# Decoder layer, tree attention: where the softmax sum is divided out, and which engine moves weights and attention row

## What is computed

```python
self_logits = jnp.einsum('bhnd,bhnd->bhn', Q, K) * scale
nbr_logits = jnp.einsum('bhld,bhlnd->bhln', Q, nk) * scale
nbr_logits = jnp.where(causal_mask[None, None], -jnp.inf, nbr_logits)
all_logits = jnp.concatenate([self_logits[..., None], nbr_logits], axis=-1)
w = jax.nn.softmax(all_logits, axis=-1)
all_v = jnp.concatenate([V[:, :, :, None, :], nv], axis=3)
out = jnp.einsum('bhln,bhlnd->bhld', w, all_v)
...
return out @ Wo.T + bo
```

## Time and profile before

| what | value |
| --- | --- |
| median of 3 runs | 2362.91 us (2362.0 to 2380.96) |
| the profiled execution | 2362.72 us, span 2360.7 us |
| busy, of the span | TensorE 2049.5 us, VectorE 1616.1, ScalarE 1072.2, GpSimd 1036.9 |
| VectorE's waits for gathered rows, 1220 to 2300 us | 128.6 us in 92 waits |

### The profile page before, as it was taken

One profiled execution on the slowest core, in us unless ns is written; L12 is line 12 of the kernel. 1 busy time (PEld: TensorE's weight loads), 2 busy tenths in 40 slices (PEclk: granted clock), 3 DMA queues, 4 the chain that ended last, 5 costly groups with the idle time before them and its releaser, 6 DMA issues.

```text
span 2360.7 us, 33037 instructions
## 1 busy us (share of the span) xinstructions
PE 2049.5 (87%) x11360; PEld 1023.6 (43%) x11360; DVE 1616.1 (68%) x2129; ACT 1072.2 (45%) x1854; POOL 1036.9 (44%) x1084
## 2 busy tenths in 40 slices
PE   4899999999999999996147888998989999988997
PEld 2333333333333333331014555555555555555555
DVE  8564647566564647552568888888888888888850
ACT  3354545455555545464013444444444444444444
POOL 3232534244352535233444464465555555455420
PEclk9999999999999999998568999999999999999999
DMA  5442434434342434331875675665665675675520
GB/s 193 146 126 73 144 97 131 145 108 152 121 149 79 142 96 130 117 108 63 311 268 186 220 235 188 220 231 199 221 236 195 215 255 195 206 249 195 199 85 18
DMA packets 188800, 392.40 MB, mean 166 GB/s; under 512 B 20692, under 2 KB 82260, under 8 KB 188632
## 3 DMA queue, kind: packets, MB, share of 16 engines
q1 hardware_dynamic: 133336, 188.91, 25.1%
q0 software_dynamic: 55296, 201.35, 24.6%
HBM read 312.33 MB, written 77.59 MB: 165 GB/s over the span
## 4 chain that ended last, share of the span: by engine, by line
DVE 28%; DMA 11%; POOL 5%; issue 4%; PE 3%; ACT 0%; DVEq 0%; SPq 0%; ACTq 0%; POOLq 0%
DMA nb<-kv_flat,idx_rows 10%; DVE bank L1497 10%; DVE logits L1444 5%; POOL nb L1568 5%; DVE nb L1493 5%; DVE nb L1435 4%; PE bank L1172 1%; PE bank L1148 1%; DMA own<-kv_flat 1%; DVE bank L1503 1%; DVE logits L1448 1%; DVE own L1439 1%; DVE total L1474 1%; DVE top L1466 1%; DVE weights L1481 0%
## 5 line engine op out<-in xcount | busy, mean ns | idle before, releaser
L712 DVE TENSOR_REDUCE neg_max<-rows_ps 128x2 f32<-128x1024 f32 x256 | 312.4, 1220 | 298.3 <-PE rows_ps L499 298.2
L1568 POOL DMA_INDIRECT nb<-kv_flat,idx_rows x384 | 366.6, 955 | 138.0 <-issue 86.2
L1435 DVE TENSOR_TENSOR nb<-nb,bank 128x1024 f32<-128x1024 f32 x192 | 231.7, 1218 | 142.5 <-DMA nb<-kv_flat,idx_rows 137.7
L627 ACT ACTIVATE probsT<-e_ps 128x1024 f32<-128x1024 f32 x256 | 262.0, 1023 | 145.1 <-PE e_ps L527 144.8
L1596 POOL TENSOR_TENSOR nb<-nb,weights 128x1024 f32<-128x1024 f32 x96 | 182.5, 1914 | 281.8 <-DVE weights L1481 281.1
L1497 DVE TENSOR_TENSOR bank<-bank,nb 128x512 f32<-128x512 f32 x384 | 268.2, 698 | 24.7 <-DVE bank L1497 0.5
L1148 PE MATMUL bank<-x2T_hi,w_hi_sb 128*128 128x256 f16 x1024 | 282.4, 276 | 0.7 <-issue 0.7
L1148 PE MATMUL bank<-x2T_lo,w_hi_sb 128*128 128x256 f16 x1024 | 281.9, 275 | 0.0
L1148 PE MATMUL bank<-x2T_hi,w_lo_sb 128*128 128x256 f16 x1024 | 281.4, 275 | 0.0
L517 PE MATMUL o_ps<-probsT,v_sb 128*33 128x512 f32 x1024 | 269.6, 605 | 6.3 <-ACT oT L624 6.1
L1444 DVE TENSOR_REDUCE logits<-nb 128x32 f32<-128x1024 f32 x192 | 230.0, 1211 | 0.0
(11 more groups left out here) (158 smaller groups left out, 3611.8 us busy)
## 6 DMA issues: line engine op xcount, KB each, us to landing
kv_flat<-kv_nat SPq DMA_DIRECT2D x128, 256.0 KB, 3.3
own<-kv_flat SPq DMA_DIRECT2D x32, 512.0 KB, 3.8
q_stack<-qk_dram SPq DMA_DIRECT2D x96, 128.0 KB, 3.0
k_stack<-qk_dram SPq DMA_DIRECT2D x96, 128.0 KB, 3.3
piece<-in_pieces SPq DMA_DIRECT2D x40, 256.0 KB, 3.5
in_sb<-in_xT SPq DMA_DIRECT2D x8, 1024.0 KB, 6.6
in_sb<-in_ctxT SPq DMA_DIRECT2D x8, 1024.0 KB, 5.6
qk_dram<-hi SPq DMA_DIRECT2D x32, 256.0 KB, 2.2
```

The costliest lines, as they stand in the source:

```text
L627: act.activation(probsT[:, (d - E_LAG) % TT, :, :], e_ps[:], ACT.Exp, scale=1.0 / (Q_UP * K_UP))\
L712: dve.tensor_reduce(neg_max[:, g % 2, at:at + 2], rows_ps[:], AX.X, ALU.max, negate=True).then_inc(max_done, 1)
L1435: dve.tensor_tensor(kk, kk, q.unsqueeze(1).to_broadcast([P, GN, D]), ALU.mult)\
L1568: pool.indirect_dma_start(nb[:, slot(lt, g), k, :], None, kv_flat, bass.IndirectOffsetOnAxis(idx_rows[:, lt, at:at + 1], 0))\
```

## The change

The weights are no longer divided by their sum. ScalarE, which makes the exponentials, also copies them to PSUM (now line 1286), waiting for itself, and this copy, no longer VectorE's in-place multiply, sends weights_ready. VectorE and GpSimd multiply the values by the exponentials as they are. VectorE computes total and its inverse behind its first value multiply, and when the row O is complete it multiplies it by the inverse into o_sb (line 1509), which takes the place of ScalarE's copy. This last step waits for all accumulations, the inverse, and TensorE's transposition of the tile before. GpSimd's and TensorE's programs are the same.

```diff
--- before.py
+++ after.py
@@ -1277,16 +1277,14 @@
                     cols = slice(lt * P, (lt + 1) * P)
                     turned_parts(b, lt, "x", x2T_hi[:, :, cols], x2T_lo[:, :, cols])
 
-                def copy_o(b, lt):
-
-                    act.wait_ge(o_part, START + (b * TT + lt + 1) * O_STEPS)
-                    act.activation(o_sb[:, lt % 2, :], O[:], ACT.Copy).then_inc(o_copied, 1)
-
                 def exponentials(b, lt):
                     act.wait_ge(shifted, START + b * TT + lt + 1)
                     act.activation(weights[:].rearrange("p n h -> p (n h)"),
                                    logits[:, lt % 2].rearrange("p n h -> p (n h)"), ACT.Exp, scale=SCALE / W_UP)\
                         .then_inc(exp_done, 1)
+                    act.wait_ge(exp_done, START + b * TT + lt + 1)
+                    act.activation(Q[lt % RT][:, 0:(NN + 1) * H], weights[:].rearrange("p n h -> p (n h)"), ACT.Copy)\
+                        .then_inc(weights_ready, 1)
 
                 def x2_sum(b, lt):
 
@@ -1385,15 +1383,10 @@
                         act.wait_ge(h_rest, START + n + 1)
                         act.activation(hid_lo[:, c % 2, :], HB[c % 2][:, 0:RW], ACT.Relu, scale=1.0 / W_UP,
                                        bias=b1_sb[:, c:c + 1]).then_inc(h_ready, 1)
-                        if attend and c + 1 == OUT_AT[0]:
-                            copy_o(ab, first)
-                        if attend and c + 1 == OUT_AT[1]:
-                            copy_o(ab, second)
 
                 for lt in range(RT):
                     turned_query(0, lt)
                 exponentials(0, 0)
-                copy_o(0, 0)
                 turned_out(0, 0)
                 x2_sum(0, 0)
                 turned_query(0, RT)
@@ -1402,7 +1395,6 @@
                 x2_apply(0, 0)
                 turned_x2(0, 0)
                 turned_query(0, RT + 1)
-                copy_o(0, 1)
                 turned_out(0, 1)
                 x2_sum(0, 1)
                 x2_square(0, 1)
@@ -1468,23 +1460,19 @@
                     dve.tensor_tensor(lg, lg, top[:].unsqueeze(1).to_broadcast([P, NN + 1, H]), ALU.subtract)\
                         .then_inc(shifted, 1)
 
-                def normalise(b, lt):
+                def totals(b, lt):
                     n = b * TT + lt
                     dve.wait_ge(exp_done, START + n + 1)
                     dve.tensor_reduce(total[:], weights[:].rearrange("p n h -> p h n"), AX.X, ALU.add)\
                         .then_inc(norm_step, 1)
-                    dve.wait_ge(norm_step, START + n * 3 + 1)
+                    dve.wait_ge(norm_step, START + n * 2 + 1)
                     dve.reciprocal(total[:], total[:]).then_inc(norm_step, 1)
-                    dve.wait_ge(norm_step, START + n * 3 + 2)
-                    shares = total[:].unsqueeze(1).to_broadcast([P, NN + 1, H])
-                    dve.tensor_tensor(weights_ps(lt), weights[:], shares, ALU.mult).then_inc(norm_step, 1)
-                    dve.tensor_tensor(weights[:], weights[:], shares, ALU.mult).then_inc(weights_ready, 1)
 
                 def values(b, lt):
 
                     n = b * TT + lt
                     w_ps = weights_ps(lt)
-                    dve.wait_ge(norm_step, START + n * 3 + 3)
+                    dve.wait_ge(weights_ready, START + n + 1)
 
                     def multiply(g):
                         dve.wait_ge(gathered[slot(lt, g)], (16 * GN) * fills(b, lt, g))
@@ -1497,6 +1485,7 @@
                         dve.tensor_tensor(O[:], O[:], nb[:, slot(lt, g), k, D:2 * D], ALU.add).then_inc(o_part, 1)
 
                     multiply(0)
+                    totals(b, lt)
 
                     if not (isinstance(b, int) and b == 0 and lt == 0):
                         dve.wait_ge(x2_summed, START + n)
@@ -1513,6 +1502,12 @@
                         if g + 1 in DVE_V_GROUPS:
                             multiply(g + 1)
                         accumulate(g, 1)
+                    dve.wait_ge(norm_step, START + n * 2 + 2)
+                    dve.wait_ge(o_part, START + (n + 1) * O_STEPS)
+                    if n:
+                        dve.wait_ge(turn_ready, START + turn_of(*last_tile(b, lt), "o") + 1)
+                    dve.tensor_tensor(o_sb[:, lt % 2, :].rearrange("p (h d) -> p h d", h=H), O[:].rearrange("p (h d) -> p h d", h=H),
+                                      total[:].unsqueeze(2).to_broadcast([P, H, DH]), ALU.mult).then_inc(o_copied, 1)
 
                 def attention(b, half, more):
 
@@ -1522,7 +1517,6 @@
                         if more or lt % RT == 0:
                             nb_, nl = next_tile(b, lt)
                             key_sums(nb_, nl, tuple(range(KEYS_AHEAD)))
-                        normalise(b, lt)
                         values(b, lt)
 
                 dve.memset(ones_rows[:], 1.0).then_inc(bias_step, 1)
```

## The result

The changed kernel took 2426.09 us, median of 4 executions (2419.98 to 2434.49), beside 2362.45 (2355.44 to 2380.96) for the kernel before on the same chip: ratio 1.0259 [1.0193, 1.0326]. Slower, where 2338 was forecast; the interval begins at 1.0193, so that it is slower is clear, that it is so by 2% is not.

| job | changed kernel, us | kernel before, us | ratio [95%] |
| --- | --- | --- | --- |
| first | 2426.09 (2419.98 to 2434.49) | 2362.45 | 1.0259 [1.0193, 1.0326] |
| fourth | 2421.99 (2413.07 to 2422.65) | 2365.93 | 1.0208 [1.0167, 1.0249] |
| fifth | 2335.99 (2333.14 to 2336.90) | 2365.06 | 0.9872 [0.9846, 0.9899] |
| sixth | 2338.74 (2333.61 to 2340.99) | 2365.77 | 0.9881 [0.9861, 0.9901] |

The account below looks back on a forecast made before the run. The loop of VectorE's weights, GpSimd's multiplies and gathers, and their landings was taken to bound the kernel. 16 x 0.66 + 14 x 1.03 = 25.0 us, plus 0.1: 2362.7 - 25.1 = 2338 us, range 2321 to 2356.

Parts of the forecast that it names:

- Sum of the gain: Gathers' loop over 30 tiles: 16 x 0.66 + 14 x 1.03 = 25.0 us, plus 0.1 in the last tile.
- First gather: GpSimd's first gather in a tile: 5.91 us after the first value multiply, 0.66 us sooner in 16 tiles, 1.03 in 14.
- Rival 3: Pause before the first gather follows the weights, so the insertion costs nothing there: 42 us gained, 2321; chance 0.10.
- The insertion: Total and reciprocal between VectorE's first value multiply and own's multiply: 0.73 us ahead of the accumulation, bounds 0.69 to 0.81.
- Rival 2: DMAs booked by other transfers: sooner gathers land no sooner, VectorE waits longer; 2363, up to 2366; chance 0.11.
- rival 1: ScalarE's queue delays the exponentials, so VectorE waits for weights: 2353 if 15 tiles wait 1 us each; chance 0.15.
- my sign of 10: VectorE's wait for ScalarE's copied weights (line 1286): near zero expected; over 10 us would mean ScalarE is late.
- The row on VectorE: Row copy moved from ScalarE to a VectorE multiply at tile end: about 0.75 us, under the wait for the next rows.
- rival 4: VectorE's reductions or key multiplies blocked by GpSimd's multiplies: 2452, or 2395 with one stall a tile; chance 0.06.
- The added wait: VectorE's wait, at the moved row multiply, for the transposition of the tile before: for something a tile old.
- neither it nor TensorE is in the loop, so zero: ScalarE saves 0.6 and adds 0.41 us per tile; no effect on time, as both engines are outside the pacing loop.
- its wait for the row gone to zero: Sign that the prediction is wrong altogether: a tile loop that TensorE ends, without its wait for the attention row.

Follow-up runs that it names:

- calm jobs: Stays on one chip in which the changed kernel or its variants ran fast; the changed kernel itself took 2336 to 2339 us there.
- disturbed: Said of the first and fourth job, in which the same changed kernel, word for word, took 2422 to 2426 us.
- row_only: Kernel before, weights normalised as ever, with VectorE copying the finished row to SBUF in place of ScalarE: 2360.52 us, ratio 1.0007.
- second: Job with four variants beside the kernel before, without the changed kernel itself; the three variants of the changed kernel took 2333.65 to 2335.02 us.

## Why the prediction was wrong, point by point

**Sum of the gain: right, in calm jobs.** 25.1 us were forecast, to 2338; the gain was 29.1 and 27.0 us in the jobs that held the changed kernel, to 2336.0 and 2338.7; the 2 to 4 us above the sum are not accounted for. In the other two calm jobs, where only variants of it ran, the gain was 24.1 to 26.6. Its terms can be read in the calm trace, VectorE and then GpSimd:

```profile
1729.88 1.21 DVE L1481 TENSOR_TENSOR nb<-nb,bank 128x1024 f32<-128x1024 f32 x1
1731.01 0.50 DVE L1466 TENSOR_REDUCE total<-weights 128x16 f32<-128x208 f32 x1
1731.54 0.25 DVE L1469 RECIPROCAL total<-total 128x16 f32<-128x16 f32 x1
1731.71 0.67 DVE L1492 TENSOR_TENSOR bank<-own,bank 128x512 f32<-128x512 f32 x1
1732.49 0.70 DVE L1485 TENSOR_TENSOR bank<-bank,nb 128x512 f32<-128x512 f32 x1
...
1743.69 0.69 DVE L1509 TENSOR_TENSOR o_sb<-bank,total 128x512 f32<-128x512 f32 x1
1744.30 1.21 DVE L1427 TENSOR_TENSOR nb<-nb,bank 128x1024 f32<-128x1024 f32 x1
1747.39 1.22 DVE L1427 TENSOR_TENSOR nb<-nb,bank 128x1024 f32<-128x1024 f32 x1 [1.88 <-DMA nb<-kv_flat,idx_rows]
```

```profile
1725.96 3.79 POOL L1590 TENSOR_TENSOR nb<-nb,weights 128x1024 f32<-128x1024 f32 x2 [3.94 <-ACT bank L1286]
1735.74 1.05 POOL L1562 DMA_INDIRECT nb<-kv_flat,idx_rows  x1 [6.00 <-DVE bank L1485]
```

- First gather: 1735.74 - 1729.88 = 5.86 us after the first multiply, 5.91 forecast. Over 30 tiles it is 5.85 to 5.88, one at 6.18, tiles with and without row numbers alike, as said; also in the disturbed trace, 5.85 to 5.89, one at 6.19. So the loop's own mechanics did not change there. What releases it is line 1485, after 6.00 us of GpSimd's idle time. Rival 3 (all 1.39 us) is out.
- The insertion: own's multiply follows the reciprocal by 0.17 us (0.2 forecast) and starts 1.83 us after the first multiply, against 1.13 in the earlier trace rows: 0.70, forecast 0.73. The 0.05 by which the gather comes sooner is there and in the accumulation behind it.
- VectorE's waits for gathers: 100.3 us, forecast about 100 (128.6 before). Rival 2 would have made them more. My argument against it was wrong all the same: the DMAs were not idle when the first gather was issued. In the kernel before, the us before the gather at 1750.70 has a DMA share of 0.93 and 285 GB/s, and the share ahead of the first gather lies between 0.07 and 1.0 by tile.
- ScalarE late (rival 1): VectorE waited for line 1286 for 0.8 us in all (8.2 us in 4 waits in the disturbed execution, under my sign of 10). ScalarE's write to PSUM, which no row of before showed, takes 348 ns in the group of 30 below; I had taken 370. GpSimd starts its multiplies up to 4.2 us before the value multiply, 3.6 us in about half of the tiles.

```profile
L1286 ACT ACTIVATE bank<-weights 128x208 f32<-128x208 f32 x30 | 10.4, 348 | 0.9
```

- The row on VectorE: 692 ns, priced by own's 0.69; row_only shows its cover by itself.
- New overlap (rival 4): key multiply and reduction keep 1.22 and 1.2 us with GpSimd's multiplies beside them (1725.96 to 1729.75 lies over the first two rows below, the second of which is two reductions). The Trainium skill (SBUF — State Buffer, "Who interferes with whom") says that reductions don't contend on this chip, and the trace now agrees, with 1212 ns as the mean of 178:

```profile
1726.48 1.22 DVE L1427 TENSOR_TENSOR nb<-nb,bank 128x1024 f32<-128x1024 f32 x1 [0.26 <-DMA nb<-kv_flat,idx_rows]
1727.62 2.34 DVE L1436 TENSOR_REDUCE logits<-nb 128x32 f32<-128x1024 f32 x2
```

```profile
L1427 DVE TENSOR_TENSOR nb<-nb,bank 128x1024 f32<-128x1024 f32 x178 | 214.8, 1218 | 101.7 <-DMA nb<-kv_flat,idx_rows 100.3 <-PE bank L1108 0.3
L1436 DVE TENSOR_REDUCE logits<-nb 128x32 f32<-128x1024 f32 x178 | 213.3, 1212 | 0.0
...
L1509 DVE TENSOR_TENSOR o_sb<-bank,total 128x512 f32<-128x512 f32 x31 | 21.5, 692 | 2.8
```

- The added wait, which I priced at zero because it is for something a tile old: zero, in two calm jobs.

**What failed**, and it decided the measured 2426, is this step: "neither it nor TensorE is in the loop, so zero: what TensorE could lose is under its 2.8 us of waiting". It takes the handover between engines as fixed (0.05 us in my sum for ScalarE). In the disturbed jobs TensorE's handovers to ScalarE did not hold to that: in the tile shown four of them took 1.7 to 4.7 us, several in a row, on the way from the transposed row through the network's chunks to the next projected query. The cover of 2.8 us a tile was used up (TensorE's wait for the row 10.9 to 15.3 us in all), TensorE's way became the loop, and VectorE waited 78.2 us for a query. The prediction's sign for this, "its wait for the row gone to zero", is nearly what the profile shows. But I gave no case and no chance to it: rival 1 has ScalarE late for the weights alone, none of the four has TensorE's way grow slower and end the loop, and the range ended at 2356 by work that the sum knew. Which of the two times is met goes by the job, of which the sum knew nothing: in the fifth and sixth job the same forecast is met.

**What stays open.** Why TensorE's updates are late in a disturbed job is not settled. That bursts begin with the gathers and keep step with them is shown; that the gathers' descriptors or landings delay the updates is only argued. A rival stands untested: the same bursts lose the trace's records, and every timed execution on record has a traced span, so the recording itself may take part in the delay. Nor is it shown that the change makes the kernel open to it. For that speaks that the kernel before, run in turn with it in both disturbed jobs, kept its median (2362.45, 2365.93) while three kernels of the changed kind were at 2422 to 2437. But no trace of it from the fourth job exists, the one trace of it is of an execution (2362.72 us) that stands in no job's list, and its single executions in these two jobs reached 2380.96 and 2377.24, where in the calm ones the highest is 2372.08; it may have the same late updates and more cover for them, since ScalarE stood waiting 124.7 us for its copy of the row. Whether the variant in which ScalarE waits, or the one without the third wait, would hold in a disturbed job wasn't seen, because neither ran in one: the wait's part there is not excluded.

## What to carry to other kernels

Run the changed kernel itself again in the same job as its variants before a difference is put down to an edit: three variants at 2334 to 2335 beside a remembered 2426 made a clean and false story, and three more at 2422 to 2437, run by themselves, seemed to confirm it. Where a wait ends at "remote", compare the end of the producing instruction with its semaphore update; if the update is late, look for what differs between the runs before you blame an edit. Where an update has no record at all, look at when its waiter started: a missing record is not yet a delay. A cover of 2.8 us a tile on an engine outside the loop is a margin against late handovers too, not only against added work.

## What the runs showed of the hardware that was not expected

- In two jobs of the four in which the changed kernel ran, about 590 of 3475 semaphore updates of the second block were recorded late or not at all. The late ones are TensorE's (125 in the first job, 3.2 us in the median); those of the other engines are missing, without a delay where it can be checked. VectorE's durations are unchanged (key multiply 1218 ns in either). The medians lie 83 to 90 us apart. In all other executions traced, every update but two is within 15 ns of its instruction's end.
- The same chip showed both in different jobs (second and fourth); within a job all 4 executions lay on the same side.
- An additional satisfied semaphore wait on VectorE cost nothing that shows in a calm job: two waits 2337.8, three 2336.0 us in the same job.
- Most of a further 692 ns instruction per tile on VectorE vanished in its waiting: 21.4 us of work, 0.07% [-0.02%, 0.17%] of time.
